# A graph network on one core: twenty source tiles gathered ahead of the first edge stage in place of twelve, and filters stored with the rows of two tiles side by side

## The reference, cut to what matters

```python
def reference(x, src, dst, edge_attr_20, edge_attr_3, edge_weight, ...):
    # 10000 nodes, 10000 edges, 512 features; dst is sorted, src is not
    # first layer: aggregate over edges, then a 512x512 product
    xp = x @ W
    msg = xp[src_all] * norm[:, None]
    out = segment_sum(msg, dst_all) + b
    x = layernorm(x + relu(out))
    # second layer
    h = shifted_softplus(f_ij @ Wf1 + bf1)
    Wf = (h @ Wf2 + bf2) * rcut_ij[:, None]      # the filter of each edge, 512 columns are used
    ...                                          # gather x[idx_j], multiply by the filter, segment_sum by idx_i
    x = layernorm(x + concat(S, V))
```

## Time and profile before

| | us |
|---|---|
| median of 3 runs | 1063.95 (1062.75 to 1065.17) |
| the profiled execution, device time | 1060.8 |
| its span, first to last instruction | 1058.7 |
| first edge stage in it, from the first scatter to the last one landed | 70.4 to 339.1 |
| PE / DVE / ACT / POOL busy over the span | 89% / 79% / 66% / 61% |

### The profile page before, as it was taken

One profiled execution on the slowest core, in us unless ns is written; L12 is line 12 of the kernel. 1 busy time (PEld: TensorE's weight loads), 2 busy tenths in 40 slices (PEclk: granted clock), 3 DMA queues, 4 the chain that ended last, 5 costly groups with the idle time before them and its releaser, 6 DMA issues.

```text
span 1058.7 us, 17984 instructions
## 1 busy us (share of the span) xinstructions
PE 943.4 (89%) x5218; PEld 767.6 (73%) x5218; DVE 837.9 (79%) x2368; ACT 703.7 (66%) x1641; POOL 642.6 (61%) x931
## 2 busy tenths in 40 slices
PE   5979999898894999999999679999999999929885
PEld 4958777776673788888888457887888888818774
DVE  5778788887662789888888758888888888817998
ACT  2668877787682466666666645666666666618997
POOL 4017888888863356666666354676666766534664
PEclk9989999999896999999999889999999999969998
DMA  9989999999998599988999586999999999768999
GB/s 346 418 303 223 247 238 237 237 238 238 231 236 192 217 321 331 331 318 318 334 327 331 223 295 166 220 227 213 206 222 229 215 206 218 122 102 329 410 416 365
DMA packets 105703, 280.43 MB, mean 265 GB/s; under 512 B 13107, under 2 KB 17479, under 8 KB 105607
## 3 DMA queue, kind: packets, MB, share of 16 engines
q1 hardware_dynamic: 68598, 191.42, 49.3%
q0 software_dynamic: 35280, 82.63, 40.7%
q10 hardware_dynamic: 1728, 5.24, 1.3%
HBM read 132.38 MB, written 146.87 MB: 264 GB/s over the span
## 4 chain that ended last, share of the span: by engine, by line
PE 55%; DMA 6%; DVE 5%; issue 2%; ACT 1%; POOL 1%; SPq 0%; DVEq 0%; POOLq 0%; ACTq 0%
PE bank L1330 14%; PE bank L1334 7%; PE bank L1378 7%; PE bank L1361 7%; PE bank L1392 5%; PE bank L1390 3%; PE bank L1321 3%; PE bank L1355 3%; DVE stat L1168 2%; PE bank L1388 2%; PE bank L1367 2%; DMA out<-R_mem 1%; DMA sum<-R_mem,l_sidx 1%; PE bank L1365 1%; PE bank L1356 1%
## 5 line engine op out<-in xcount | busy, mean ns | idle before, releaser
L552 POOL DMA_INDIRECT sum<-R_mem,sidx_all x79 | 131.3, 1662 | 91.1 <-DMA sum<-zeros 49.3
L613 POOL DMA_INDIRECT sum<-R_mem,l_sidx x79 | 134.6, 1704 | 48.3 <-DMA sum<-R_mem,l_sidx 25.3
L1330 PE MATMUL bank<-G_hi 128*128 128x512 f32 x316 | 130.4, 413 | 0.0
L599 POOL DMA_INDIRECT G_mem<-x_d,dst_i x79 | 77.3, 979 | 87.3 <-PE bank L1365 61.5
L1330 PE MATMUL bank<-G_lo,G_hi 128*128 128x512 f32 x316 | 124.2, 393 | 0.0
L1244 PE MATMUL bank<-G_hi,M_mem 128*128 128x512 f32 x200 | 85.4, 427 | 9.4 <-ACT R_mem L685 9.4
L1334 PE MATMUL bank<-G_hi,G_lo 128*128 128x512 f32 x316 | 85.3, 392 | 0.0
L1119 DVE SCALAR_TENSOR_TENSOR edge_mem<-edge_mem,Y,bank 128x128 f32<-128x128 f32 x237 | 71.2, 385 | 15.1 <-ACT edge_mem L806 14.1
L1361 PE MATMUL bank<-edge_mem,Winv 128*128 128x512 f32 x158 | 81.8, 600 | 0.1
L1244 PE MATMUL bank<-G_lo,M_mem 128*128 128x512 f32 x200 | 79.6, 398 | 0.0
L1255 PE MATMUL bank<-edge_mem,Wf_s 128*128 128x256 f32 x320 | 78.6, 390 | 0.7 <-ACT node_mem L679 0.7
(11 more groups left out here) (263 smaller groups left out, 2921.2 us busy)
## 6 DMA issues: line engine op xcount, KB each, us to landing
node_mem<-sum SPq DMA_DIRECT2D x41, 512.0 KB, 5.9
filt_d<-node_mem SPq DMA_DIRECT2D x40, 512.0 KB
node_mem<-filt_d SPq DMA_DIRECT2D x79, 256.0 KB
sum<-zeros SPq DMA_DIRECT2D x33, 512.0 KB
G_mem<-x SPq DMA_DIRECT2D x20, 512.0 KB, 6.3
x_d<-node_mem SPq DMA_DIRECT2D x20, 512.0 KB, 2.9
sum<-node_mem SPq DMA_DIRECT2D x20, 512.0 KB, 4.5
edge_mem<-x SPq DMA_DIRECT2D x19, 512.0 KB, 6.3
```

The source lines that it names most:

```text
L552: pool.indirect_dma_start(sum0, bass.IndirectOffsetOnAxis(ap=sidx[:, t:t + 1], axis=0), R[t % 8][:, :], None, compute_op=ALU.add).then_inc ...
L599: pool.indirect_dma_start(G3[t % 8][:, :], None, x1_d, bass.IndirectOffsetOnAxis(ap=dst_i[:, t:t + 1], axis=0)) \
L613: pool.indirect_dma_start(sum1, bass.IndirectOffsetOnAxis(ap=l1_sidx[0:n, t:t + 1], axis=0), R3[t % 8][0:n, :], None, compute_op=ALU.add). ...
L1330: pe.matmul(bank[4 + a][:, :], zT_hi[a][:, c * P:(c + 1) * P], w[c][:, :], start=(c == 0 and w is W0h), stop=False)
```

## The change

Two things change, both in the first edge stage.

**Gathers.** The ring `G0` gets eight more buffers, in columns 2048 to 6143 of `keep`, so `NG` is 20. POOL issues the first twelve gathers as before, then waits until `w_pre` has reached 1, and issues eight more before it waits for the zero stores. After the scatters of group g it now gathers for the group five ahead. ACT and DVE read the ring's new places; the gathers count on five semaphores in place of three.

**Filters.** `filt_pair` replaces `pair_rows`: row 2p of the 256 is the first tile's row p, row 2p + 1 the second tile's. A partition's two pieces are then 4 KB in one run. The load of one tile takes every second row.

```diff
-        NG = 12
-        G0 = G + [b[:, 2 * D:3 * D] for b in node_mem]
+        NG = 20
+        G0 = G + [b[:, 2 * D:3 * D] for b in node_mem] + views(4 * D, 8, D, keep)
...
+        def filt_pair(i):
+            return filt_d[i * 256:(i + 1) * 256, :].rearrange("(p v) d -> p v d", v=2)
...
-                        sp_.dma_start(pair_rows(filt_d, i, 0, D), wst[i % 4]).then_inc(w_st[i % 4], 16)
+                        sp_.dma_start(filt_pair(i), wst[i % 4]).then_inc(w_st[i % 4], 16)
...
-                sp_.dma_start(filt[t % 4], rows(filt_d, t)).then_inc(f_filt[t % 4], 16)
+                sp_.dma_start(filt[t % 4], filt_pair(t // 2)[:, t % 2, :]).then_inc(f_filt[t % 4], 16)
...
             for t in range(NG):
+                if t == 12:
+                    pool.wait_ge(w_pre, 1)
                 gather0(t)
```

More of the change, by code:

```diff
@@ L104, in rows @@
     return dram[bass.ds(t * P, P), :]
-def pair_rows(dram, s, c0, c1):
-    return dram[bass.ds(s * 2 * P, 2 * P), c0:c1].rearrange("(k p) d -> p k d", p=P)
 def layer_pair(dram, j, c0, c1):
```

## The result

| | before | changed |
|---|---|---|
| median of 5 runs each, one after the other (us) | 1062.94 | 1069.95 |
| lowest and highest | 1062.2 to 1065.17 | 1067.49 to 1074.41 |
| ratio, 95% interval | | 1.0072 (1.0045 to 1.0098) |
| the profiled execution, device time | 1060.8 | 1074.4 |
| its span | 1058.7 | 1072.4 |

The change costs 7.0 us by the medians; I had forecast 1061.6 us, a gain, with a range up to 1065.5. The profiled execution of the changed kernel is the slowest of its five, so its rows tell where time goes better than how much. The gather is L534 now (it was L536), `fT` L428 and the filter store L432; L552, L685 and L1283 keep their numbers.

The account below looks back on a forecast made before the run. It took POOL's issuing (13.4 us a group) as the bound, the scatter-landing chain (12.6 us) just under. Tail -1.9, start +0.3 and filter stores -0.7 summed to -2.3 us: 1061.6 us for the median, range 1057 to 1065.5.

Parts of the forecast that it names:

- What bounds the kernel now: First edge stage: POOL's issuing, 13.4 us a group, sets the pace; the chain of scatter and landing, 12.6 us, lies just under.
- cover: Stage start: slack ahead of the fourth scatter; zeros could land up to 77.4, 7.0 us later, without moving it.
- The eight gathers at the start: From about 59 us: eight extra gathers delay the zeros to 75.4 to 75.7; taken at +0.3 us, between 0 and +1.
- The margin of 2 us for `fT`: Stage start: `fT` for step 2 lands at 75.8 to 76.1, PE uses it at 78.06.
- the start slips: Rival, stage start: late zeros and `fT` delay the fourth scatter by 3.5 us, time some 1065 or 1067.5; chance 0.14.
- The schedule of groups 0 to 13 doesn't change at all: First edge stage, groups 0 to 13: still four scatters and four gathers each, only for a later group; no gain there.
- Nothing is bought by: Longer lead: ACT's waits for gathers go, but POOL was not waiting for ACT; taken at 0, bounds 0 and 0.7 us.
- The tail: Five periods from group 14 to 19: fewer gathers, so each takes the landing chain's 12.64 us; 63.2 for 65.1, -1.9 us.
- Filter stores: Stores in 4 KB runs take 0.15 us less per group, counted in the five last periods: -0.7 us, bounds 0 and -3.0.
- Filter loads: 79 loads read every second row, still 2 KB in a run; taken at 0.
- signs of being wrong: Periods of groups 1 to 13 under 13.2, fourth scatter past 83.5, PE waiting for `fT` near 78, longer second edge stage.
- The pacer rival: First edge stage: the DMA engines set the pace, so work taken off them counts in full; -8.3 us, 1055.7; chance 0.20.

Follow-up runs that it names:

- a1: Kernel before with only the longer gather ring (twenty gathers ahead), filters stored and loaded as before: 1067.0 us, ratio 1.0037.
- c1: Kernel before with twenty gathers ahead, old filter layout, ACT also waiting for the next group's gathers: 1067.43 us, ratio 1.0075.
- c0: The kernel before, unchanged, profiled again on another chip; the median of before in that batch was 1058.8 us.
- c3: Kernel before with twenty gathers ahead and no filter stores (rows of `x` loaded in place of filters): ratio 1.0028.
- c2: Kernel before without the 40 filter stores, twelve gathers ahead (rows of `x` loaded in place of filters): ratio 0.9989.
- a2: Kernel before with only the new filter layout (4 KB runs in the store), twelve gathers ahead: 1066.44 us, ratio 1.0034.
- a5: Kernel before with the filters' new places in DRAM, each pair stored as two transfers in 2 KB runs, twelve gathers ahead: ratio 1.0008.
- d2: Kernel before with twenty gathers ahead, old filter layout, and `W0` loaded behind the `fT` of steps 2 and 3: ratio 1.0069.
- d1: Kernel before with only the four `W0` loads moved behind the `fT` of steps 2 and 3, twelve gathers: 1056.14 us, ratio 0.9975.
- e3: Kernel before with twenty gathers, old filter layout, `W0` behind `fT`, ACT held by next group's gathers, `x` loaded behind the last scatter: ratio 1.0003.
- f2: The kernel of e3 run again on one more chip, without the pause, against the kernel before: ratio 1.0040.

## Why the prediction was wrong

In the profiled execution the first edge stage lost 9.6 us where the sum had a gain of 2.3. Of that the groups behind the start, priced at 0, lost 5.2; the last four periods 2.4; the start, priced at +0.3, lost 2.0. No rival had the first of these.

**"What bounds the kernel now": right, but read from one kind of start.** Scatter and landing do lie just under POOL's issuing; the waits behind group 15 appeared, and ACT's waits changed from gathers to scatters as I said. What I could not see in one profile is that its engines paused in the set-up, and that the "cover" of 7 us ahead of the fourth scatter was that pause.

**"The eight gathers at the start", +0.3 us: the term that was mis-sized.** The zeros landed at 74.7, I had 75.4 to 75.7: the bytes were priced well. The cover was not. The margin of 2 us for `fT` is the sentence that failed: I had it at 75.8 to 76.1, it landed just before 78.7, and PE waited 2.07 us. What I left out altogether is what PE does behind such a wait: 0.66 us of the loss is the later product, 1.2 us the sums at a clock of 0.53. The term measured 2.0 us in the changed kernel and 0.8 in a1, with the pause, and 7.6 to 8.2 without it (c1 against c0, c3 against c2). This is the rival "the start slips", though not by its own condition, zeros later than 77.4; it needed no more than the forecast 5 us, since `fT` decided. I gave it 0.14.

**"The schedule of groups 0 to 13 doesn't change at all": wrong.** The order didn't, the timing did. The middle lost 5.2 us in the changed kernel; 1.6 in a1 by the lead and 2.4 in a2 by the runs of 4 KB, which leaves 1.2 that neither half shows alone. "Nothing is bought by" the longer lead was the right remark, and 0 was the wrong price: an ACT that no longer waits for gathers has its filters, and so their stores, ready at another time (c1 takes away the one, c3 the other).

**The tail, -1.9 us: the mechanism right, the sum not.** POOL does stand and wait for landings behind groups 15 to 18, but a period bound by landing is hardly shorter than one bound by POOL. Without stores c3 against c2 shows -1.1, not clear of chance; with filter stores in the periods the last four are +2.4 (changed) and +3.2 (a1). Two steps failed. I took 12.64 us as the period without gathers and passed over the one beside it, 303.68 to 316.99 in the earlier trace rows, 13.31 us and with no gather behind its scatters either; with the mean of the two, 13.0, five periods give 64.9 in place of 65.1, which is nothing. And the last pair of stores and the load of `x` meet in the last period, which was 15.4 us in a1 and 13.8 in the changed kernel.

**"Filter stores", -0.7 us: the wrong sign.** I compared rates of transfers and asked how soon the store is done. What counts is how long it keeps the scatters from landing: +3.7 us in a2. Both the row that I priced by and the packet overhead ask about the store itself.

**Filter loads, at 0:** held as far as can be told. a5 reads them in the new places and is the same as before, within -1.0 and +2.8 us. The second edge stage was 2.8 us longer in the changed kernel, one of the signs of being wrong that I had named; that the loads did it isn't shown.

The pacer rival is out: a2 moved the same bytes in half the packets and lost, and c2, without the stores' 8.8 MB in the first window, gained nothing that can be measured.

## What to carry to other kernels

Work that is added where an engine idles still has to find room on the DMA engines: price its bytes against what is in flight, and then ask of each small transfer in the same stretch who waits for it. A small load that the critical engine needs goes ahead of large ones that nobody needs yet; here that was worth 2.8 and 3.2 us with nothing else changed, on two chips without the pause. When PE has to wait, look at its clock behind the wait as well. Before a stretch of idle time counts as cover, look at a second profile, on another chip if there is one. And where a latency is the bound, judge the transfers beside it by what they do to that latency, not by their own rate.

## What the runs showed of the hardware

- A store of 512 KB in runs of 4 KB lengthens the landing of 2 KB accumulating rows beside it: 6.1 and 6.5 us of wait against 5.3 and 5.7 with 2 KB. 1 KB gives no more (5.1 and 6.3). With no stores in c3 it is 4.5 to 4.8 us, except before group 19 (6.8), where a load of `x` runs beside.
- The same program has two kinds of start, apart by some 6 us of pauses near 16 to 22 us. Each batch, which is one chip, showed one kind in all its profiles; what causes it stays open, and no run was made for it.
- Once the DMA engines are full (share 1.02 to 1.03 up to 70 us), a small load issued from 56.5 us was there at 75.4 (d2), and no later than 70.5 with 2.1 MB less in flight (d1).
- A PE that stood for 7.2 us was at 1.2 GHz for the 8 us behind it (c3, 0.50). In the changed kernel PE stood for 2.07 us, and from 81 to 84 us its clock was 0.53 where it was 1.00 before: there this cost 1.2 us, more than the later product's 0.66.
- Left open: that e3 tied where f2 lost 4.5 us goes by the pause alone in my reading, with one chip of each kind; and the 4 us behind the stage in the changed kernel's profile.
